# A two-layer cross-attention and FFN kernel: two engines' work in another order in each attention slot, and another opening

## The chip, the cores and the metric

The kernel runs on one NeuronCore of a Trainium2 chip, in one launch. The metric is the device time of that launch in microseconds (us). The engines are PE (TensorE, the matrix engine), DVE (VectorE), ACT (ScalarE), POOL (GpSimd) and SP (SyncE, which here only issues DMA transfers). Each runs its own list of instructions in program order, and they meet at semaphores: an instruction adds to a counter when it is done, and a `wait_ge` holds an engine's list until a counter has a value. TensorE's clock has two levels, 1.2 and 2.4 GHz; the profile gives the granted one as a share of the full one.

## The reference

Eight batches of 256 tokens with 128 features go through two layers. Every sublayer reads the layer norm of the residual x and is added to x.

```python
x = x + L0_xattn(_layernorm(x), ctx_1024, ctx_1024, ...)   # 16 heads of 8 features, 256 x 256 scores per head
x = x + L0_ffn(_layernorm(x), ...)                         # 8 experts, top 1 by a softmax gate: silu(x W1 + b1) W2 + b2
x = x + L1_xattn(_layernorm(x), ctx_1024, ctx_1024, ...)   # 16 heads, no biases, position bias slope * distance, mask
x = x + L1_ffn(_layernorm(x), ...)                         # square(relu(x W_fc.T)) W_proj.T, then 5 spiking steps
```

One attention, cut down:

```python
wq, wk, wv = (q @ Wq.T + bq), (k @ Wk.T + bk), (v @ Wv.T + bv)      # split into 16 heads of 8
probs = softmax(einsum('bthd,bshd->bhts', wq, wk) / sqrt(8))
out = einsum('bhts,bshd->bthd', probs, wv).reshape(b, t, d) @ Wo.T + bo
```

## The kernel before

The order in time is: loads and an opening, the attention of layer 0, the gate and the sorting of tokens by expert, the experts, the attention of layer 1, the second FFN. The two attentions are one piece of code (`attention_on_tensor`, `attention_on_scalar`, `attention_on_vector`, `attention_on_gpsimd`, `attention_on_sync`), built with `ly["bias"]` true for layer 0 and `ly["position"]` true for layer 1.

**Slots.** An attention is a software pipeline written out by hand. `slots_loop` calls `slot_fn` for the slots s = -3 to 8. In slot s, batch b = s is `cur` (its second score pass, the exponentials and the products with the values), batch s + 1 is `nxt` (its first score pass and the maxima over keys), the projections of batch s + 2 are made (`new`), and the output of batch s - 1 is finished (`old`). Nothing but this hand-written order, on each engine, and the semaphores set who goes first. `new` ends with slot 5, `nxt` with slot 6.

**A slot on PE.** `pair(0)` to `pair(7)` are the score products of two heads each, of `nxt` (line 292, into S1) and of `cur` (line 301, into S2). Between them stand: `m_turn` (line 352, turns the row maxima `mparts` so that they can be written as rows of the query tile), `pv` (line 343, probabilities times values, four groups per batch; group 3 of a batch falls into the next slot), the turn of the outputs `Osb` (line 382), the turn of the normed x (line 406), the query product (415), the key product (421), the turn of the normalised output `attn` (426), the output projection (434) and the value product (445). Small results share two PSUM banks, M[0] and M[1], which is why many of them wait for the copy of the one before.

**A slot on ACT.** `exp(0)` to `exp(7)` (line 508) read S2. Between them ACT copies small results out of PSUM: `m_copy` (516), `o_copy` (495), `xnT` (532), `qf` and `q_hi` (538, 543: the queries in float32 and their float16 high part), `kf` and `k_hi` (479, 484, in `keys_on_scalar`), `aT` (558) and the values `Vt` (568).

**DVE and POOL.** DVE makes the 16 maxima of `nxt` (line 651, two per `r(i)`), turns them into `mparts` in layer 0 (`shift`, line 659), normalises outputs (`o_norm`), adds the projected output to X (740), and makes the sums of the layer norm. POOL takes the norm's root (627), applies the norm (620), makes the low parts `q_lo` and `k_lo` (805, 763), and in layer 0 adds the output bias to X (815). In layer 1 POOL makes `mparts` from the maxima in five steps (`parts`, 775 to 783), and in slots 0 to 3 `mix_on_gpsimd` (1330, 1333) adds the experts' result for batch s + 4 to X, as the last thing of the slot.

**Opening.** SP loads the context, the key weights, the first two batches of X in one transfer, the query weights, then the other six batches and two more weights; ACT loads `qkb` (biases), `eye`, `rows` and `ob`. Six of these count into `loaded`. PE and DVE wait for all six. DVE clears tiles first, then scales the biases and makes the norm's sums; POOL clears `pos_parts` (needed in slot 4), applies the norm of the first batches and makes `q_lo` of batch 0. The first score products need the whole query tile of batch 0, whose low part is the last to arrive.

Of the kernel before, what the change touches and what calls it, by code (L numbers as in the profile page):

```python
# [33 lines left out]
P = 128  # L34
# [71 lines left out]
def build(nc, t, out):  # L106

    with ExitStack() as ctx:
# [75 lines left out]
        loaded, loaded_x, loaded_late, pos_stored = sem("loaded"), sem("loaded_x"), sem("loaded_late"), sem("pos_stored")  # L184
        inited, zeroed = sem("inited"), sem("zeroed")
        N_LOADS, N_LOADS_X, N_LATE = 6, 4, 22
        N_PARTS_MADE = 8
        INIT_KEYS, INIT_TILES, INIT_SECOND, N_INIT = 14, 17, 22, 25
# [95 lines left out]

        def attention_on_tensor(pe, ly, masked, ffn=None):
# [50 lines left out]
            def pv(b, par, g):  # L336
# [19 lines left out]
            def slot_fn(b, par, s):  # L356
# [51 lines left out]
                if ly["bias"]:  # L408
                    outputs_turn()
# [7 lines left out]
                pair(3)  # L417
                if new and not keys_ahead(ly, s):
# [73 lines left out]
        def attention_on_scalar(act, ly, ffn=None):  # L492
# [5 lines left out]
            def slot_fn(b, par, s):  # L498
# [20 lines left out]
                if cur and ly["bias"]:  # L519
                    m_copy(b, 1)  # L520
# [4 lines left out]
                if cur and ly["position"]:  # L525
                    m_copy(b, 1)
# [1095 lines left out]
```

## Time and profile before

| | |
|---|---|
| median of three runs | 433.56 us (433.47 to 438.4) |
| the profiled execution | 437.06 us |
| its span in the trace | 434.8 us |
| mean granted clock of TensorE | 0.872 |
| PE busy | 338.6 us (78%) |
| DVE busy | 297.0 us (68%) |
| ACT busy | 253.3 us (58%) |
| POOL busy | 152.4 us (35%) |

The span starts with the first instruction and ends with the last. Busy times include overlap with other engines, so no share by itself says what ends a stage. Per stage, read as "what did the engine that is waited for wait for", the chain of waits and the idle time before each instruction tell more.

### The profile page before, as it was taken

The numbers are of one execution on the slowest core, as the hardware profiler recorded it, in microseconds if no ns is written. First come the engines' busy times: TensorE is split into PE (matmuls) and PEld (weight loads), VectorE is DVE, ScalarE is ACT, GpSimd is POOL, SyncE is SP. The second block draws the span as 40 slices with busy tenths as digits, with TensorE's granted clock in tenths as the row PEclk, the third lists the DMA queues.
The fourth block names the chain that finished last, engine by engine and source line by source line (L and its number), as shares of the span: only waits on it lengthen the run. The fifth ranks groups of instructions, "written<-read, shape, count | busy, mean of one in ns | idle before, by whom it ended". The sixth has DMA issues, their size and how long they took to land.

```text
span 434.8 us, 9212 instructions
## 1 busy us (share of the span) xinstructions
PE 338.6 (78%) x3164; PEld 195.4 (45%) x3164; DVE 297.0 (68%) x762; ACT 253.3 (58%) x436; POOL 152.4 (35%) x255
## 2 busy tenths in 40 slices
PE   1499998879988934999941759889789888968882
PEld 0133344434443522998940213434434443457771
DVE  5677888888774666466614766878787873238885
ACT  2128878877668310665521137768777867457772
POOL 3431333245200205654027364445354210444500
PEclk9999999999888765899985555998998978789997
DMA  4214432333111041354212122112111100000001
GB/s 145 60 55 136 139 85 90 98 84 80 59 54 55 11 149 34 112 158 123 45 51 66 51 64 68 29 51 60 49 32 58 56 5 6 2 2 0 24 26 48
DMA packets 36062, 27.37 MB, mean 63 GB/s; under 512 B 6080, under 2 KB 32064, under 8 KB 36016
## 3 DMA queue, kind: packets, MB, share of 16 engines
q1 hardware_dynamic: 33040, 23.55, 18.7%
q0 software_dynamic: 1248, 2.56, 2.8%
q10 hardware_dynamic: 1728, 0.66, 0.6%
q8 instruction: 28, 0.46, 0.4%
q14 instruction: 18, 0.15, 0.1%
HBM read 14.22 MB, written 4.13 MB: 42 GB/s over the span
## 4 chain that ended last, share of the span: by engine, by line
PE 48%; DVE 20%; POOL 10%; issue 10%; ACT 6%; DMA 4%; SPq 1%; POOLq 0%; ACTq 0%; DVEq 0%
PE M L343 11%; DVE nm L651 9%; PE S L292 9%; PE S L1232 5%; PE S L1251 5%; PE M L434 3%; PE M L445 2%; DVE tmp L1364 2%; PE M L415 2%; POOL xn L620 2%; PE M L352 2%; DVE Pt L1367 2%; POOL w_ff L1148 2%; PE M L1420 1%; DMA wq<-in_wq 1%
## 5 line engine op out<-in xcount | busy, mean ns | idle before, releaser
L651 DVE TENSOR_REDUCE nm<-S 128x2 f32<-128x512 f32 x256 | 164.6, 688 | 44.4 <-PE S L292 37.9
L508 ACT ACTIVATE Pt<-S 128x1024 f32<-128x1024 f32 x128 | 130.2, 1019 | 43.0 <-PE S L301 40.5
L292 PE MATMUL S<-Kt,Qt 32*128 32x256 f16 x512 | 84.8, 309 | 17.2 <-DVE nm L651 6.2
L301 PE MATMUL S<-Qt,Kt 32*128 32x256 f16 x512 | 77.5, 299 | 0.7 <-ACT Pt L508 0.7
L343 PE MATMUL M<-Pt,Vt 128*32 128x256 f32 x1024 | 76.4, 421 | 0.1
L292 PEld LDWEIGHTS S<-Kt,Qt 32*128 32x128 f16 x512 | 23.1, 95 | 79.3 <-DVE nm L651 53.9
L627 POOL TENSOR_TENSOR rstd<-ve,mhalf 128x2 f32<-128x2 f32 x24 | 17.5, 728 | 67.9 <-DVE ve L605 67.7
L343 PEld LDWEIGHTS M<-Pt,Vt 128*32 128x32 f32 x1024 | 28.7, 117 | 27.6 <-issue 13.6
L1279 ACT ACTIVATE hf<-S,b1c 128x128 f32<-128x128 f32 x92 | 26.3, 368 | 18.3 <-PE S L1232 17.0
L805 POOL TENSOR_TENSOR q_lo<-qf,q_hi 128x256 f16<-128x256 f32 x15 | 10.2, 678 | 67.5 <-ACT q_hi L543 49.5
L1141 POOL DMA_INDIRECT xt<-normed_x,source x23 | 22.2, 967 | 20.1 <-PE M L1242 13.5
L1232 PE MATMUL S<-x_t,w_t 128*128 128x128 f32 x184 | 27.0, 293 | 0.7 <-DVE x_t L1302 0.5
L1251 PE MATMUL S<-w_ff,hf 128*128 x184 | 24.3, 276 | 0.9 <-issue 0.9
L301 PEld LDWEIGHTS S<-Qt,Kt 32*128 32x128 f16 x512 | 21.7, 95 | 6.3 <-ACT Pt L508 3.8
L1232 PEld LDWEIGHTS S<-x_t,w_t 128*128 128x128 f32 x184 | 23.8, 202 | 1.7 <-issue 1.4
L532 ACT ACTIVATE xnT<-M 128x256 f32<-128x256 f32 x16 | 6.1, 382 | 28.8 <-PE M L406 28.8
L1251 PEld LDWEIGHTS S<-w_ff,hf 128*128 128x128 f32 x184 | 22.4, 192 | 1.2 <-issue 1.2
L1148 POOL DMA_INDIRECT w_ff<-sorted_y,slot x16 | 15.6, 974 | 20.5 <-DMA sorted_y<-ysb 16.2
L620 POOL TENSOR_SCALAR xn<-X,mv,rstd 128x128 f32<-128x128 f32 x28 | 22.2, 798 | 1.4
L434 PE MATMUL M<-wo,aT 128*128 128x128 f32 x64 | 13.8, 348 | 8.7 <-ACT aT L558 8.7
L516 ACT ACTIVATE mT<-M 64x256 f16<-64x256 f16 x32 | 11.9, 373 | 14.1 <-PE M L352 14.1
L352 PE MATMUL M<-eye,mparts 128*64 128x128 f16 x64 | 10.4, 251 | 12.2 <-POOL mparts L783 8.9
(174 smaller groups left out, 542.6 us busy)
## 6 DMA issues: line engine op xcount, KB each, us to landing
w_ff<-in_w SPq DMA_DIRECT2D x8, 512.0 KB, 4.0
ctxT<-in_ctxT SPq DMA_DIRECT2D x16, 128.0 KB, 2.6
Pt<-in_mask SPq DMA_DIRECT2D x8, 256.0 KB
Qt<-q_hi SPq DMA_DIRECT2D x28, 64.0 KB, 1.9
Kt<-k_hi SPq DMA_DIRECT2D x28, 64.0 KB, 1.9
sorted_y<-ysb SPq DMA_DIRECT2D x23, 64.0 KB
Kt<-k_lo SPq DMA_DIRECT2D x16, 64.0 KB, 1.9
Qt<-q_const SPq DMA_DIRECT2D x16, 64.0 KB, 3.5
```

The lines of the kernel that those rows point to most:

```text
L292: mm = pe.matmul(S1[h % 2][:, q, :], Qt[b % NBUF][rows_of(h), h // HG, q * P:(q + 1) * P], Kt[b % NBUF][rows_of(h), h // HG, :], start=Tru ...
L301: mm = pe.matmul(S2[pair % 2][:, hh, k, :], Kt[b % NBUF][rows_of(h), h // HG, k * P:(k + 1) * P], Qt[b % NBUF][rows_of(h), h // HG, :], st ...
L343: mm = pe.matmul(M[1][KB * i:KB * i + KB, tile * S:(tile + 1) * S], Vflat[par][:, at:at + KB], Pt[g][:, i, k * S:(k + 1) * S], start=(sub ...
L434: mm = pe.matmul(M[1][:, q * D:(q + 1) * D], aT[:, q * P:(q + 1) * P], W["o", ly["index"]][:, :], start=True, stop=True)
L508: act.activation(Pt[i // 2][:, 2 * j:2 * j + 2, :].rearrange("p a n -> p (a n)"), S2[i % 2][:, :, :, :].rearrange("p a k n -> p (a k n)"), ...
L620: i = pool.tensor_scalar(xn[par][:, q, :], X[:, b * QT + q, :], mv[:, q, 0:1], rstd[:, q:q + 1], ALU.subtract, ALU.mult)
L651: v.tensor_reduce(nm[par][:, h // 8, :, h % HG, h // HG % 2], S1[h % 2][:, :, :], AX.X, ALU.max, negate=True)\
L1141: pool.indirect_dma_start(xt[j % XT_BUFS][:, :], None, xn_dram, bass.IndirectOffsetOnAxis(ap=source[:, j:j + 1].bitcast(U32), axis=0)) \
L1148: pool.indirect_dma_start(yg[:, i, :], None, ys_dram, bass.IndirectOffsetOnAxis(ap=slot[:, i:i + 1].bitcast(U32), axis=0)) \
L1232: mm = pe.matmul(S2[j % H_BUFS // 2][:, j % 2, c // 2, (c % 2) * P:(c % 2 + 1) * P], w1_t[j % X_BUFS][:, c, :], x_t[j % X_BUFS][:, :], sta ...
L1251: pe.matmul(o, hf[j % HF_BUFS][:, c * P:(c + 1) * P], second_weights(e, c), start=(c == 0), stop=False)
L1279: i = act.activation(hf[j % HF_BUFS][:, c * P:(c + 1) * P], S2[j % H_BUFS // 2][:, j % 2, c // 2, (c % 2) * P:(c % 2 + 1) * P], ACT.Silu, ...
```

## The change

The table of the slots is changed in five places, the opening in four.

- PE, layer 0: `m_turn(b, 1)` goes behind `pv(b - 1, 3)`, as it stood in layer 1; ACT's `m_copy(b, 1)` goes behind `o_copy` with it. The turn of the outputs goes ahead of that of the normed x.
- PE, both layers: the turn of `attn` goes ahead of the key product. ACT, both layers: the copy `aT` goes ahead of `kf` and `k_hi`.
- The last batch's `pv` accumulates in M[0] and waits for the maxima's copy, no longer for `x_added`.
- POOL, layer 1: `mix_on_gpsimd` stands right behind `parts(b, 1)` at the start of the slot instead of at its end.
- Opening: X of batch 0 is SP's first transfer, X of batch 1 another; the key weights and `rows` come first on ACT's queue, `qkb` fourth; `loaded` counts five transfers. DVE makes the norm's sums of batch 0 before it waits for `loaded`, applies the norm of batches 0 and 1 and makes `q_lo` of batch 0. POOL clears the value tiles `Vt` (`clear_values`) instead of DVE, and clears `pos_parts` behind slot 0 of layer 0 (`clear_positions`).

The core of the diff:

```diff
-        INIT_KEYS, INIT_TILES, INIT_SECOND, N_INIT = 14, 17, 22, 25
+        INIT_KEYS, INIT_TILES, INIT_SECOND, N_INIT = 12, 15, 19, 21
...
+        def o_bank(b):
+            return M[0] if b == B - 1 else M[1]
...
                 if cur:
-                    if old:
+                    if s == B - 1:
+                        pe.wait_ge(ly["mT_copied"], 2 * B)
+                    elif old:
                         pe.wait_ge(ly["x_added"], b)
...
         def first_tiles_on_vector(v):
+            v.wait_ge(loaded, 16 * N_LOADS)
+            v.tensor_scalar(qkbs[:, 0:1], qkb[:, 0:1], QK / float(np.sqrt(DH)), None, ALU.mult).then_inc(inited, 1)
+            v.tensor_scalar(qkbs[:, 1:2], qkb[:, 1:2], QK, None, ALU.mult).then_inc(inited, 1)
             v.tensor_scalar(Kt[0][:, :, :], Kt[0][:, :, :], rows[:, 0:1], None, ALU.add).then_inc(inited, 1)
+            v.tensor_scalar(vb[:, :], ones32[:, :], qkb[:, 2:3], None, ALU.mult).then_inc(inited, 1)
...
+                    if s == -3 and ly["bias"]:
+                        first_tiles_on_vector(v)
                     if s < -1:
                         norm_apply(v, b + 3, xn[1 - par], ly["xrstd"], ly["xn_ready"])
+                    if s == -3 and ly["bias"]:
+                        v.wait_ge(loaded_x1, 16)
+                        norm_sums(v, 1, ly["norm_own"])
...
+        def clear_values(pool, i):
+            pool.memset(Vt[i][:, :, :, :], 0.0).then_inc(cleared, 1)
+            pool.wait_ge(cleared, 2 * i + 1)
+            pool.memset(Vheads[i][:, :, :, DH], 1.0).then_inc(cleared, 1)
+
+        def clear_positions(pool):
+            pool.memset(pos_parts[:, :, :], 0.0).then_inc(zeroed, 1)
+            pool.wait_ge(zeroed, 1)
+            pool.memset(pos_parts[:, 0:PARTS, :], MROW).then_inc(zeroed, 1)
...
                 if cur and ly["position"]:
                     parts(b, par, 1)
+                    if s < B - MIX:
+                        mix_on_gpsimd(pool, b + MIX)
...
             first = QT * 2
+            sp.dma_start(X[:, 0:QT, :], t["x"][:, 0:QT, :]).then_inc(loaded_x0, 16)
             context_on_sync(sp, ly[0], -2, 0)
-            for dst, src in [(W["k", 0][:, :], t["wk0"]), (X[:, 0:first, :], t["x"][:, 0:first, :]), (W["q", 0][:, :], t["wq0"])]:
-                sp.dma_start(dst, src).then_inc(loaded, 16)
+            sp.dma_start(W["q", 0][:, :], t["wq0"]).then_inc(loaded, 16)
+            sp.dma_start(X[:, QT:first, :], t["x"][:, QT:first, :]).then_inc(loaded_x1, 16)
...
-            for dst, src in [(qkb[:, :], t["qkb"]), (eye[:, :], t["c_eye"]), (rows[:, :], t["c_rows"])]:
+            for dst, src in [(rows[:, :], t["c_rows"]), (W["k", 0][:, :], t["wk0"]), (eye[:, :], t["c_eye"]), (qkb[:, :], t["qkb"])]:
                 act.dma_start(dst, src).then_inc(loaded, 16)
```

ACT's list in slot 1 of layer 0, from the copy of the queries to that of the values, before:

```order
L538 ACTIVATE qf<-M,qkbs 128x256 [waits L0_q_lo,L0_q_done]
L543 ACTIVATE q_hi<-qf 128x256 [waits L0_q_tile,L0_q_copied]
L508 ACTIVATE Pt<-S_1 128x1024 [waits L0_p2_done]
L479 ACTIVATE kf<-M,qkbs 128x256 [waits L0_k_lo,L0_k_done]
L484 ACTIVATE k_hi<-kf 128x256 [waits L0_k_rep,L0_k_copied]
L558 ACTIVATE aT<-M 128x256 [waits L0_aT_done]
L508 ACTIVATE Pt<-S_0 128x1024 [waits L0_p2_done,L0_pv_done]
L568 ACTIVATE Vt<-M 128x8x4x8 [waits L0_pv_done,L0_v_done]
```

And after the change:

```order
L533 ACTIVATE qf<-M,qkbs 128x256 [waits L0_q_lo,L0_q_done]
L538 ACTIVATE q_hi<-qf 128x256 [waits L0_q_tile,L0_q_copied]
L505 ACTIVATE Pt<-S_1 128x1024 [waits L0_p2_done]
L551 ACTIVATE aT<-M 128x256 [waits L0_aT_done]
L476 ACTIVATE kf<-M,qkbs 128x256 [waits L0_k_lo,L0_k_done]
L481 ACTIVATE k_hi<-kf 128x256 [waits L0_k_rep,L0_k_copied]
L505 ACTIVATE Pt<-S_0 128x1024 [waits L0_p2_done,L0_pv_done]
L563 ACTIVATE Vt<-M 128x8x4x8 [waits L0_pv_done,L0_v_done]
```

`aT`, which PE's output projection waits for, has moved ahead of two copies; the exponential behind them has the same three copies ahead of it.

POOL's list in layer 1 from the norm of one slot to the next slot's `q_lo`, before (rows 1330 and 1333 are the mix, 775 to 783 the parts of the next slot):

```order
L620 TENSOR_SCALAR xn<-X,mv,rstd 128x128 [waits L1_xnT_done,L1_xrstd]
L620 TENSOR_SCALAR xn<-X,mv,rstd 128x128
L1330 TENSOR_TENSOR w_ff<-w_ff,gate 128x256
L1333 TENSOR_TENSOR X<-X,w_ff 128x256 [waits moe_scaled]
L775 TENSOR_SCALAR mr<-nm 128x16 [waits L1_mT_done,L1_max_done]
L777 CAST mparts<-mr 128x8x2 [waits L1_own]
L779 TENSOR_TENSOR mr<-mr,mparts 128x16 [waits L1_own]
L781 CAST mparts<-mr 128x8x2 [waits L1_own]
L783 TENSOR_TENSOR mparts<-mr,mparts 128x8x2 [waits L1_own]
L805 TENSOR_TENSOR q_lo<-qf,q_hi 128x256 [waits L1_q_hi,L1_q_tile]
```

And after:

```order
L615 TENSOR_SCALAR xn<-X,mv,rstd 128x128 [waits L1_xnT_done,L1_xrstd]
L615 TENSOR_SCALAR xn<-X,mv,rstd 128x128
L783 TENSOR_SCALAR mr<-nm 128x16 [waits L1_mT_done,L1_max_done]
L785 CAST mparts<-mr 128x8x2 [waits L1_own]
L787 TENSOR_TENSOR mr<-mr,mparts 128x16 [waits L1_own]
L789 CAST mparts<-mr 128x8x2 [waits L1_own]
L791 TENSOR_TENSOR mparts<-mr,mparts 128x8x2 [waits L1_own]
L1343 TENSOR_TENSOR w_ff<-w_ff,gate 128x256
L1346 TENSOR_TENSOR X<-X,w_ff 128x256 [waits moe_scaled]
L818 TENSOR_TENSOR q_lo<-qf,q_hi 128x256 [waits L1_q_hi,L1_q_tile]
```

The five steps now stand ahead of the mix.

DVE's list in the opening of layer 0, from the norm of batch 0 to the tiles of the other buffers, after the change (before, `xn` and `q_lo` are not on DVE, and the wait for `loaded` stands ahead of the norm's sums):

```order
L597 BN_AGGR mv<-st 128x2 x2
L600 TENSOR_SCALAR ve<-mv 128x2 [waits L0_norm_own]
L627 TENSOR_SCALAR qkbs<-qkb 128x1 [waits loaded]
L628 TENSOR_SCALAR qkbs<-qkb 128x1
L629 TENSOR_SCALAR Kt<-Kt,rows 128x1024
L630 TENSOR_SCALAR vb<-ones,qkb 128x128
L631 TENSOR_SCALAR q_const<-q_const,rows 32x1024
L605 TENSOR_SCALAR xn<-X,mv,rstd 128x128 [waits L0_xrstd]
L605 TENSOR_SCALAR xn<-X,mv,rstd 128x128
L588 BN_STATS st<-X 128x6 [waits loaded_x1]
```

`xn` of batch 0 is made on DVE behind five instructions that wait for the loads.

## Rows read from the trace of the kernel before

**Rows 1.** The page, part 1: engine, busy us (share of the span), instructions.

```profile
PE 338.6 (78%) x3164; PEld 195.4 (45%) x3164; DVE 297.0 (68%) x762; ACT 253.3 (58%) x436; POOL 152.4 (35%) x255
```

**Rows 2.** The chain that ended last, both openings: start us, us, what.

```profile
2.11 5.62 DMA wq<-in_wq
...
10.17 1.59 POOL xn L620 x2
15.23 0.80 POOL q_lo L805
16.05 1.93 DMA Qt<-q_lo
...
236.19 0.43 DVE q_lo L708
```

**Rows 3.** The DMA view, 0 to 20 us: issues, sizes, us to landing.

```profile
ob<-in_ob ACTq DMA_DIRECT2D x1, 64.0 KB, 5.5
...
rows<-in_c_rows ACTq DMA_DIRECT2D x1, 1.5 KB, 3.4
```

**Rows 4.** The timeline of the opening: start us, us, engine, line, operation.

```profile
0.72 1.80 POOL L1506 MEMSET pos_parts<- 128x2048 f16 x1 [0.29 <-POOLq L1615]
...
10.04 1.28 ACTq L490 DMA_DIRECT2D Kt<-k_hi  x2
...
12.54 0.38 ACT L532 ACTIVATE xnT<-M 128x256 f32<-128x256 f32 x1 [2.52 <-PE M L406]
...
14.73 0.42 ACT L543 ACTIVATE q_hi<-qf 128x256 f16<-128x256 f32 x1
...
18.02 0.61 PE L292 MATMUL S<-Kt,Qt 32*128 32x256 f16 x4 [3.41 <-DMA Qt<-q_lo]
```

**Rows 5.** The timeline of ACT, layer 0, slots 1 and 2.

```profile
55.67 0.38 ACT L568 ACTIVATE Vt<-M 128x256 f32<-128x256 f32 x1 [0.33 <-PE M L445]
...
68.04 0.37 ACT L558 ACTIVATE aT<-M 128x256 f32<-128x256 f32 x1
```

**Rows 6.** The timeline of PE, layer 0, slot 2.

```profile
61.07 0.27 PE L352 MATMUL M<-eye,mparts 128*64 128x128 f16 x2 [0.23 <-DVE mparts L659]
...
68.45 0.71 PE L434 MATMUL M<-wo,aT 128*128 128x128 f32 x4 [0.72 <-ACT aT L558]
```

**Rows 7.** Who waited for whom, PE, 46 to 146 us: us in total, times, longest.

```profile
PE M L434 <- ACT aT L558: 4.3, 6, 0.7
PE M L352 <- DVE mparts L659: 1.8, 4, 1.1
```

**Rows 8.** The timeline of DVE and POOL around the ends of slots 0 and 3 of layer 0.

```profile
46.71 0.18 DVE L659 TENSOR_SCALAR mparts<-nm 128x16 f16<-128x16 f32 x1
...
88.38 1.38 DVE L659 TENSOR_SCALAR mparts<-nm 128x16 f16<-128x16 f32 x1
...
88.78 0.96 POOL L1074 MEMSET b2rows<- 128x1024 f16 x1
```

**Rows 9.** The timeline of layer 1 around the start of slot 4.

```profile
315.10 2.63 DVE L651 TENSOR_REDUCE nm<-S 128x2 f32<-128x512 f32 x4
...
318.20 0.74 POOL L1333 TENSOR_TENSOR X<-X,w_ff 128x256 f32<-128x256 f32 x1
319.03 0.20 POOL L775 TENSOR_SCALAR mr<-nm 128x16 f32<-128x16 f32 x1
...
320.53 0.27 PE L352 MATMUL M<-eye,mparts 128*64 128x128 f16 x2 [1.35 <-POOL mparts L783]
...
321.15 2.49 DVE L651 TENSOR_REDUCE nm<-S 128x2 f32<-128x512 f32 x4 [1.27 <-PE S L292]
```

**Rows 10.** The timeline of PE: one group of `pv` at either clock.

```profile
142.26 1.94 PE L343 MATMUL M<-Pt,Vt 128*32 128x256 f32 x16
...
315.01 1.07 PE L343 MATMUL M<-Pt,Vt 128*32 128x256 f32 x16
```

**Rows 11.** One stretch: window, length, busy us of PE, PEld, DVE, ACT, POOL; clock; DMA.

```profile
267.00:270.00 3.00, 3.00 (x31) 1.06 (x34) 1.69 (x7) 1.72 (x4) 0.88 (x2) 0.50 0.33 96
```

More of the change, by code:

```diff
@@ L391, in slot_fn @@
                     ffn_start(ffn, -2)
-                if ly["position"]:
-                    maxima_turn()
+                if cur:
+                    pe.wait_ge(ly["v_copied"], b + 1)
+                    m_turn(b, par, 1)
                 pair(1)
-                if ly["position"]:
-                    outputs_turn()
+                if old:
+                    pe.wait_ge(ly["o_copied"], b)
+                    if s == B:
+                        pe.wait_ge(ly["x_added"], B - 1)
+                    for n in range(QT * NPK):
+                        q, tile = n // NPK, n % NPK
+                        mm = pe.transpose(M[1][:, n * P:(n + 1) * P], Osb[par1][:, tile, q * P:(q + 1) * P], eye[:, :])
+                    mm.then_inc(ly["ot_done"], 1)
                 if new:
@@ L417, in slot_fn @@
                 pair(3)
+                if old:
+                    pe.wait_ge(ly["ot_norm"], b)
+                    for q in range(QT):
+                        mm = pe.transpose(M[1][:, q * P:(q + 1) * P], attn[:, q, :], eye[:, :])
+                    mm.then_inc(ly["aT_done"], 1)
                 if new and not keys_ahead(ly, s):
@@ L524, in slot_fn @@
                     ffn_start(ffn, -2)
-                if cur and ly["position"]:
+                if cur:
                     m_copy(b, 1)
@@ L548, in slot_fn @@
                 exp(3)
-                if new and not keys_ahead(ly, s):
-                    keys_on_scalar(act, ly, b, nxt)
                 gate = s == B and ly["bias"]
@@ L560, in slot_fn @@
                     gate_copies(act, 2, GATE_AHEAD)
+                if new and not keys_ahead(ly, s):
+                    keys_on_scalar(act, ly, b, nxt)
                 exp(4)
@@ L563, in slot_fn @@
                     act.wait_ge(ly["v_done"], b + 2)
-                    if b == -1:
-                        act.wait_ge(inited, N_INIT)
+                    if b <= 0 and ly["bias"]:
+                        act.wait_ge(cleared, 2 * (b + 2))
                     if old:
@@ L694, in slot_fn @@
                     v.wait_ge(loaded_x, 16 * N_LOADS_X)
-                if ly["position"] and s < 0:
-                    if s == -1:
+                if s < 0:
+                    if s == -1 and ly["position"]:
                         add_experts(v, 2)
@@ L712, in slot_fn @@
                     norm_sums(v, b + 3, ly["norm_own"])
-                elif ahead:
-                    norm_stats(v, b + 3, ly["norm_own"], ly["xvar"], applied(b + 3))
-                if s == -3 and ly["bias"]:
-                    first_tiles_on_vector(v)
                 if s == -1 and ly["bias"]:
@@ L821, in slot_fn @@
                     gather(pool, 2 * QT + 8, NT)
-                if ly["position"] and 0 <= s < B - MIX:
-                    mix_on_gpsimd(pool, b + MIX)
             def slot_and_small_parts(b, par, s):
                 slot_fn(b, par, s)
+                if s == 0 and ly["bias"]:
+                    clear_positions(pool)
                 if s == 3 and ly["bias"]:
@@ L1505, in _ @@
         def _(pool):
-            pool.memset(pos_parts[:, :, :], 0.0).then_inc(zeroed, 1)
-            pool.wait_ge(zeroed, 1)
-            pool.memset(pos_parts[:, 0:PARTS, :], MROW).then_inc(zeroed, 1)
+            clear_values(pool, 0)
             attention_on_gpsimd(pool, ly[0])
```

49 lines of the change are left out of this document (12 added, 37 removed).

## The prediction

> **What bounds the kernel now.** I read the page's busy shares first [rows 1]. No engine is full: PE 78% of the span, DVE 68%. So an idle gap that sits on the path is worth its length, and busy work taken off an engine is worth nothing by itself. Then I read the chain of waits, which names what ended last, stage by stage, and then the timeline around each instruction that moves. Three places matter.
>
> In the opening the chain is one serial string: the loads until 7.73 (2.11 + 5.62), the norm and its application on POOL (1.59), the low part of the queries on POOL (0.80) and its transfer (1.93) [rows 2], and the first score products start at 18.02 [rows 4].
>
> In a slot of layer 0 PE stands still twice: 0.23 before the turn of the maxima and 0.72 before the output projection [rows 6]. Over the layer the first makes 1.8 us in 4 waits, one of them 1.1, the second 4.3 us in 6 [rows 7].
>
> In layer 1 the turn of the maxima waits 1.35 for POOL, and DVE then waits 1.27 for PE [rows 9].
>
> **The opening.** Call T the moment when `loaded` is complete, 7.7 before. Behind T ACT's list decides, and both ends of each step are in rows 4. ACT issues two transfers from 10.04 for 1.28 (to 11.32), and only then copies `xnT`; before, that copy starts at 12.54, since POOL's `xn` ends at 11.76 (10.17 + 1.59) [rows 2]. After, DVE makes `xn`. In front of it stand five instructions behind `loaded`, for which I take about 1.2 us (an estimate from their sizes: two of them are passes over float16 tiles like the ones cleared here), and the two halves take about 0.5, so `xn` is there at T + 1.7, the turn on PE at T + 2.5, and ACT is free at T + 3.6. The copy starts there instead of at T + 4.8: a gain of 1.2. The second step is `q_lo`. It ran from 15.23 to 16.03 on POOL, behind a `q_hi` that ended at 15.15. DVE does the same subtraction in layer 1's opening in 0.43 [rows 2] instead of 0.80, a gain of 0.3, of which the other two transfers, which ACT issues, leave all but a little: second issue plus 1.9 us lands within 0.1 of it. Sum 1.5.
>
> T itself: the query weights move one place forward, but `qkb` becomes ACT's fourth transfer, in the place of `ob`, which took 5.5 us from an issue at 2.14 and so landed at 7.6; the third, `rows`, took 3.4 [rows 3]. So T lies between some 5.5 (as quick as `rows`) and 7.7 (as `ob`). The transfer of 768 KB that slowed `ob` keeps its place, so I take the late end, 7.4: a gain of 0.3, with 2.2 as the other end. DMA: Bandwidth & Descriptors of the Trainium skill (Queues, rings and completion order) says that a semaphore's increment lands only after every earlier write of that DMA engine, on all its queues. By that, a 1.5 KB transfer issued here lands no sooner than a 64 KB one; `ob`'s row agrees, and the gain would be 0.
>
> What moved to POOL in the opening is hidden: its memset of 2048 columns took 1.80 and started at 0.72 [rows 4]; the one of 1152 columns of float32 costs between 1.0 (by columns) and 2.0 (by bytes), and POOL has nothing to do before the root at T or so. If the second clearing is late, the value copy of slot -1, ten microseconds later, covers it. DVE's tiles for the other buffers now stand behind `q_lo`; they take some 2.7 us, and end just as the first maxima become possible. Opening: **-1.8**.
>
> **Layer 0.** First, `aT`. ACT makes `kf` and `k_hi` first and starts `aT` at 68.04 [rows 5]; PE waits until 68.45 for it [rows 6]. With `aT` first PE's 0.72 goes. What is late next is the exponential behind it: it has the same three copies ahead of it and so starts at the same time, and the value copy `Vt` comes after it. That copy had waited 0.33 for PE [rows 5]. So only 0.33 of the 0.72 reaches the end of the slot. This holds in slots 1 to 5, where key products exist; slot 7 has only the wait, which stays. 5 x 0.33 = 1.65. `k_hi` comes 0.37 later, and SP waits for it; but SP is issuing the query's transfers until then, and its own keys are wanted over 4 us later, so I take 0.
>
> Second, the turn of the maxima behind `pv`. The 0.23 waits and the slack of the exponential give 0.15 in each of the other slots, some 6 x 0.15 = 0.9. The long one is of another kind: `mparts`, a DVE instruction of 0.18, took 1.38 in slot 4 and ended at 89.76, as POOL's memset did (88.78 + 0.96) [rows 8]. With a `pv` of 1.07 [rows 10] ahead of it, PE's 1.1 us are hidden: 0.9.
>
> Third, a cost. `clear_positions` now puts 1.80 + 0.74 us of memset on POOL right where slot 1 begins, and `mparts` of slot 1 at 46.71 [rows 8] falls into it. By the row of slot 4 it ends when the memset does. The turn waits 0.4 beyond `pv` if only for the first memset, 1.2 if for both; I take 0.7, and between 0 and 1.2 for the range. SBUF — State Buffer of the Trainium skill (Who interferes with whom) says the same: GpSimd and a VectorE instruction that needs the shared port pair exclude each other for a whole instruction. It speaks against this move. The two slot-4 rows agree.
>
> The turn of the outputs ahead of the norm's gives DVE its input 0.4 earlier, but now waits for `o_copied` some 0.2: 0. Layer 0: -1.65 - 0.9 - 0.9 + 0.7 = **-2.75**.
>
> **Layer 1.** The maxima of slot 4 are complete at 317.73 (315.10 + 2.63), but POOL is in the mix until 318.94 and starts `parts` at 319.03; PE turns at 320.53 [rows 9]. With `parts` first it starts at about 317.8, 1.2 earlier. PE's `pv` ends at 319.2, so the turn comes right behind it. DVE's 1.27 of idle time [rows 9] lets it follow, and ACT was idle too, so the 1.2 survives to the second exponential. The mix falls at the ends of slots 0 to 3; slot 1's `parts` were late by DVE and not by the mix, so three slots gain: 3 x 1.2 = 3.6. The mix itself (1.4 us) now lies in POOL's idle 4.5 us before `q_lo`, and DVE's sums need the mix of the slot before. In slot 0 it waits for the gathered rows, beside nothing. `aT` as in layer 0: 5 x 0.33 = 1.65. The last batch's bank removes a wait that was nearly over: 0. Layer 1: **-5.25**.
>
> Sum: -1.8 - 2.75 - 5.25 = **-9.8 us**. Made against the profiled execution, 437.06 (span 434.8) to 427.3. That execution was 3.5 above the median, by TensorE's clock, I take it, and the saving does not depend on that: 433.56 - 9.8 = **423.8**. About 2% (8.7 us) is what a measurement of this kernel can tell from no change.
>
> **Rivals.**
>
> *Half of it is given back (428.5).* PE and DVE hand the two S1 banks to and fro, and DVE has only about 1 us free in a slot of 14. If the small gains of 0.15 and 0.33 are lost there (all of 2.55 in layer 0 and 1.65 in layer 1) and the stall of slot 1 takes 1.2, then 9.8 - 4.2 - 0.5 = 5.1 is left: 428.5. For it: DVE's gaps are short. Against it: two of them, in front of the sum and of the next maxima, are just those that `aT` ends. Chance 0.22.
>
> *The clock falls less often, or T comes early (419.5).* TensorE's granted clock falls to half several times in both attentions, after slots in which PE had idle time, and `pv` then takes 1.94 instead of 1.07 [rows 10]. A slot has four of them. If one slot in each layer keeps its clock, some 2 us each; with T at 5.5, 2.2: 423.8 - 4.3 = 419.5. TensorE: Matmul & The Clock Gate of the Trainium skill (Part 1) says that activity releases the clock; the gaps removed here would help. Chance 0.16.
>
> *The clock stays at half for longer (over 433.6: slower).* Layer 1 starts at half clock, with PE busy in 3.00 of 3.00 us at 267 to 270 and the clock at 0.50 of the full one [rows 11]. If the new phase of the work moves that release by slots, each slot costs at least 4 x 0.87 for `pv` [rows 10] and some 2 for projections, 5.5 us less 1 of slack, 4.5. From 9.8 / 4.5 = 2.2 slots on, the gain is gone; three slots give 437, and 442.3, a loss of 2%, needs four. For it: that stretch is 48 us long already. Against it: PE gets busier, not idler. Chance 0.04.
>
> *The change doesn't do what it says.* The opening could be tied to another load and the mix to its gathers, so that only the `aT` terms are left, -3.3: 430. Chance 0.05.
>
> **How the numbers follow.** The forecast has 0.53, with its own range of 421.5 to 426.5 from the bounds of T (-1.9, +0.3), of the memset (-0.7, +0.5) and of the slots. The range of all reaches to both neighbours: 418.5 to 430; above and below lie the slower case and the tails. Faster by over 2% means under 424.9: most of the forecast (0.38) and the clock case (0.16), 0.54. Slower by over 2%: half of the slow case, 0.02. Within: 0.44.
>
> **What the profile after would show.** First score products at about 16.2, with `xnT` behind ACT's two transfers; `loaded` ended by a transfer on ACT's queue; the output projection without its wait for `aT` in slots 1 to 5, and `Vt` without its wait for PE; no wait of 1.1 for `mparts` in slot 4, but one in slot 1 beside the memset; in layer 1 `parts` right behind the maxima and slots 2 to 4 shorter by 1.5. Wrong would be: slots of unchanged length with the waits elsewhere (DVE for S1, ACT for `o_copied`), or a longer stretch at half clock.

## The result and the profile after

The changed kernel takes 420.64 us (median of four runs, 419.66 to 423.13) against 435.7 for the kernel before in the same comparison: a ratio of 0.966, 95% interval 0.9575 to 0.9746, so 11 to 18.5 us faster. Measured again beside three other kernels it took 421.16, ratio 0.968 (0.963 to 0.974). The ratios leave out two single runs that lie over 1.5% above the fastest of their kernel: 432.35 of `p_keys` and 441.24 of the kernel before. The profiled execution took 419.95 (span 417.8, mean granted clock 0.887), that of before 437.06.

The page, part 1, of the changed kernel, answers to [rows 1]: PE and DVE have nearly the same work (4.1 and 2.4 us less busy time) in a span that is 17 us shorter.

```profile
PE 334.5 (80%) x3164; PEld 193.5 (46%) x3164; DVE 294.6 (71%) x763; ACT 250.2 (60%) x436; POOL 151.0 (36%) x254
```

**The opening** [rows 2 to 4]. The chain of the changed kernel (start, length, what), and then its timeline:

```profile
2.14 3.81 DMA qkb<-in_qkb
...
12.81 2.06 DMA Qt<-q_hi
```

```profile
7.08 0.59 DVE L605 TENSOR_SCALAR xn<-X,mv,rstd 128x128 f32<-128x128 f32 x2
...
8.27 1.28 ACTq L487 DMA_DIRECT2D Kt<-k_hi  x2
...
9.59 0.38 ACT L527 ACTIVATE xnT<-M 128x256 f32<-128x256 f32 x1 [1.36 <-PE M L403]
...
12.24 0.42 DVE L710 TENSOR_TENSOR q_lo<-qf,q_hi 128x256 f16<-128x256 f32 x1 [1.31 <-ACT q_hi L538]
...
14.91 0.61 PE L297 MATMUL S<-Kt,Qt 32*128 32x256 f16 x4 [3.24 <-DMA Qt<-q_hi]
```

`loaded` is complete at 5.95 (2.14 + 3.81), not at 7.73. Behind it `xnT` starts 3.64 later, behind ACT's two transfers, and the first scores 8.96 later, where before it was 10.29. So of the 3.11 gained, 1.8 are T and 1.3 what follows it.

**A slot of layer 0** [rows 5, 6]: ACT, DVE and PE in slot 2.

```profile
64.68 0.38 ACT L551 ACTIVATE aT<-M 128x256 f32<-128x256 f32 x1
...
65.11 0.71 PE L429 MATMUL M<-wo,aT 128*128 128x128 f32 x4
...
66.05 0.41 DVE L738 TENSOR_TENSOR X<-M,X 128x256 f32<-128x256 f32 x1
66.63 1.29 DVE L648 TENSOR_REDUCE nm<-S 128x2 f32<-128x512 f32 x2 [0.17 <-PE S L297]
66.67 0.38 ACT L563 ACTIVATE Vt<-M 128x256 f32<-128x256 f32 x1
67.11 0.30 PE L357 MATMUL M<-eye,mparts 128*64 128x128 f16 x2 [0.50 <-ACT Vt L563]
```

PE's output projection and ACT's `Vt` have no brackets now: nobody waits there. PE has a new wait, 0.50 for `Vt` in front of the turn of the first half of the next batch's maxima. (The other turn has none in slots 1 and 2, at 59.49 and 72.77. It waits for `v_copied` where it waited for `mT_copied`, an edit that the list of the change doesn't name.) Over the layer (PE's waits from 40 to 142: total, times, longest; compare [rows 7]):

```profile
PE M L357 <- ACT Vt L563: 2.5, 5, 0.5
PE M L416 <- DVE attn L668: 2.1, 7, 0.3
...
PE M L429 <- ACT aT L551: 0.7, 1, 0.7
```

**The start of slot 1**, where POOL's memset now lies beside `mparts` [rows 8]:

```profile
43.35 1.81 POOL L763 MEMSET pos_parts<- 128x2048 f16 x1
...
44.89 0.30 DVE L656 TENSOR_SCALAR mparts<-nm 128x16 f16<-128x16 f32 x1
```

`mparts` ends at 45.19, as the memset does (45.16), but PE is in `pv` until 46.3 and waits for nothing.

**Layer 1**, the starts of slot 4 and of slot 5 [rows 9]:

```profile
304.49 0.20 POOL L783 TENSOR_SCALAR mr<-nm 128x16 f32<-128x16 f32 x1 [0.53 <-DVE nm L648]
...
305.99 0.27 PE L357 MATMUL M<-eye,mparts 128*64 128x128 f16 x2
...
319.04 0.26 PE L297 MATMUL S<-Kt,Qt 32*128 32x256 f16 x1 [1.27 <-DMA Qt<-mT]
```

POOL now waits 0.53 for DVE's maxima, where before it was still in the mix when they were complete, and PE's turn has no wait. But slot 5 begins with a wait that before had none: 1.27 for the transfer of the maxima's row, which the chain has with 4.02 us.

**Where the time went.** The start of the output projection marks each slot. The table has, for the two profiled executions, the lead of the changed kernel there, and the length of the slots (a star marks one that holds more than 1 us at half of TensorE's full clock).

| | lead, us | slots before | slots after |
|---|---|---|---|
| first scores | 3.11 | | |
| layer 0, slot 1 | 2.64 | | |
| slots 1 to 5 | 6.34 | 13.97, 13.99, 14.86, 13.98 | 13.27, 13.28, 13.28, 13.27 |
| slots 5 to 8 | 8.40 | 14.46\*, 12.74\*, 12.80\* | 13.07, 12.72\*, 12.15\* |
| layer 1, slot 1 | 9.95 | | |
| slots 1 to 5 | 15.58 | 15.24\*, 14.90, 14.92, 14.93\* | 13.26, 13.25, 13.26, 14.59 |
| slots 5 to 8 | 17.20 | 13.12, 13.81\*, 13.59\* | 13.20\*, 13.19\*, 12.51\* |

Laid out in order of time, the lead of the two profiled executions grows by 3.1 in the opening, shrinks by 0.5 until slot 1, grows by 5.8 from slot 1 to 8 of layer 0, by 1.6 until slot 1 of layer 1, and by 7.25 from there to slot 8. The opening and the slots that hold no such stretch in either kernel (1 to 5 of layer 0, 2 to 4 of layer 1) make 3.1 + 3.7 + 3.3 = 10.1 us; in the rest the clock may have a part. The forecast had nothing for the 1.6 between slot 8 of layer 0 and slot 1 of layer 1.

### The profile page after: what moved, and what is told of

Its sections match the earlier page's. It is cut to its first block, busy times and chain, and to the rows that moved or that the text cites. A ratio compares the mean times of both kernels' runs of the same rounds, so it can differ in the third digit from the quotient of the medians.

```text
span 417.8 us, 9215 instructions
## 1 busy us (share of the span) xinstructions
PE 334.5 (80%) x3164; PEld 193.5 (46%) x3164; DVE 294.6 (71%) x763; ACT 250.2 (60%) x436; POOL 151.0 (36%) x254
## 3 DMA queue, kind: packets, MB, share of 16 engines
HBM read 14.22 MB, written 4.13 MB: 44 GB/s over the span
## 4 chain that ended last, share of the span: by engine, by line
PE 45%; DVE 16%; ACT 12%; issue 10%; DMA 7%; POOL 5%; SPq 2%; ACTq 1%; POOLq 0%; DVEq 0%
PE M L348 13%; PE S L297 10%; ACT Pt L505 5%; PE S L1245 4%; PE S L1264 4%; DVE nm L648 3%; DVE tmp L1377 3%; DVE Pt L1380 2%; DMA Qt<-q_const 2%; DMA sorted_y<-ysb 2%; PE M L410 2%; POOL w_ff L1161 2%; PE M L1433 2%; PE M L357 1%; PE M L440 1%
## 5 line engine op out<-in xcount | busy, mean ns | idle before, releaser
L297 PE MATMUL S<-Kt,Qt 32*128 32x256 f16 x512 | 86.0, 305 | 16.2 <-DMA Qt<-q_hi 7.1
L348 PE MATMUL M<-Pt,Vt 128*32 128x256 f32 x1024 | 74.9, 414 | 0.2
L615 POOL TENSOR_SCALAR xn<-X,mv,rstd 128x128 f32<-128x128 f32 x24 | 19.0, 798 | 1.2
L1377 DVE SCALAR_TENSOR_TENSOR tmp<-Pt 128x256 f32<-128x256 f32 x32 | 13.7, 428 | 7.1 <-ACT Pt L1477 6.3
L1321 DVE COPY ysb<-S 128x128 f32<-128x128 f32 x23 | 6.6, 288 | 16.6 <-PE S L1265 8.3
```

The source lines that it names most:

```text
L297: mm = pe.matmul(S1[h % 2][:, q, :], Qt[b % NBUF][rows_of(h), h // HG, q * P:(q + 1) * P], Kt[b % NBUF][rows_of(h), h // HG, :], start=Tru ...
L348: mm = pe.matmul(o_bank(b)[KB * i:KB * i + KB, tile * S:(tile + 1) * S], Vflat[par][:, at:at + KB], Pt[g][:, i, k * S:(k + 1) * S], start= ...
L615: i = pool.tensor_scalar(xn[par][:, q, :], X[:, b * QT + q, :], mv[:, q, 0:1], rstd[:, q:q + 1], ALU.subtract, ALU.mult)
L1377: v.scalar_tensor_tensor(tmp[:, :], mem[par][:, k - 1, :], BETA, mem[par][:, 0, :], ALU.mult, ALU.add) \
```

## The experiments

**One part at a time.** Four kernels start from the one before.

`p_keys` moves these lines of PE ahead of the key product, and `keys_on_scalar` on ACT behind `aT`:

```diff
+                if old:
+                    pe.wait_ge(ly["ot_norm"], b)
+                    for q in range(QT):
+                        mm = pe.transpose(M[1][:, q * P:(q + 1) * P], attn[:, q, :], eye[:, :])
+                    mm.then_inc(ly["aT_done"], 1)
                 if new and not keys_ahead(ly, s):
                     pe.wait_ge(ly["q_copied"], b + 3)
```

> The kernel before with one part of the change: the turn of attn ahead of the key product on PE, aT ahead of kf and k_hi on ACT, in both layers. Theory A (the prediction's term): 0.33 of the 0.72 survives in each of 10 slots, -3.3 us, slots of layer 0 shorter by 0.33. Theory B (the whole wait survives, because the value copy's place in the queue was never the next limit): 0.7 in each of 10 slots, -7 us, slots of layer 0 of 13.3 instead of 13.98. If the slots stay at 13.98, both fall.

Measured: 426.8 (425.89 to 432.35) against 435.6, ratio 0.979 (0.973 to 0.985), a gain of 6 to 12. Ordinary slots of layer 0 take 13.27 and 13.28 instead of 13.98; in layer 1 14.15 and 14.26 instead of 14.90. Theory B: all of the wait survives. Why, is to be seen in slot 2. The timeline of ACT and DVE there, before:

```profile
66.31 1.01 ACT L508 ACTIVATE Pt<-S 128x1024 f32<-128x1024 f32 x1
...
68.30 1.02 ACT L508 ACTIVATE Pt<-S 128x1024 f32<-128x1024 f32 x1
...
69.20 0.42 DVE L740 TENSOR_TENSOR X<-M,X 128x256 f32<-128x256 f32 x1 [0.52 <-PE M L434]
...
69.97 1.29 DVE L651 TENSOR_REDUCE nm<-S 128x2 f32<-128x512 f32 x2 [0.34 <-PE S L292]
```

And in `p_keys`:

```profile
65.45 1.01 ACT L508 ACTIVATE Pt<-S 128x1024 f32<-128x1024 f32 x1
...
66.83 0.71 PE L434 MATMUL M<-wo,aT 128*128 128x128 f32 x4
...
67.44 1.00 ACT L508 ACTIVATE Pt<-S 128x1024 f32<-128x1024 f32 x1
67.77 0.41 DVE L740 TENSOR_TENSOR X<-M,X 128x256 f32<-128x256 f32 x1
68.35 1.29 DVE L651 TENSOR_REDUCE nm<-S 128x2 f32<-128x512 f32 x2 [0.17 <-PE S L292]
```

From one exponential to the next it is 1.99 in both: on ACT nothing is gained there, as I had said. But DVE's sum, which before waited 0.52 for the projection, and the maxima behind it come 0.76 earlier behind the same exponential (2.90 instead of 3.66). So the 0.71 follows DVE's string. In front of the turn of the maxima `p_keys` has PE's wait for `Vt` already (0.45 at 55.51).

`p_turns`, layer 0 alone:

```diff
                 pair(0)
-                if ly["bias"]:
-                    maxima_turn()
                 if old:
                     pv(b - 1, par1, 3)
...
-                if ly["position"]:
-                    maxima_turn()
+                maxima_turn()
                 pair(1)
-                if ly["position"]:
-                    outputs_turn()
+                outputs_turn()
...
-                if ly["bias"]:
-                    outputs_turn()
```

> The kernel before with one part: in layer 0 the turn of the maxima behind pv (m_copy behind o_copy) and the turn of the outputs ahead of that of the normed x. Theory A (the prediction's terms): 0.15 in each of 6 slots and 0.9 in slot 4, -1.8 us. Theory B (only the stall of slot 4 counts, ordinary slots end with the wait for aT as before): -0.9 us, ordinary slots of layer 0 unchanged at 13.98 and slot 4 at 13.98 instead of 14.86.

Measured: 432.19 (430.65 to 436.02), ratio 0.993 (0.986 to 1.000). Ordinary slots take 13.70 and 13.72, 0.27 less, slot 4 takes 13.85, 1.0 less: theory A, a little larger. PE's wait for `aT` stayed what it was in these slots, 0.73 where it was 0.72, and was 0.86 in one: alone, the turn gains in front of that wait and doesn't need the other part. From slot 1 to 2 it takes 15.01: from 55 to 59 TensorE was granted 0.57, and that stretch cost 1.3.

`p_mix`:

```diff
                     parts(b, par, 1)
+                    if s < B - MIX:
+                        mix_on_gpsimd(pool, b + MIX)
...
-                if ly["position"] and 0 <= s < B - MIX:
-                    mix_on_gpsimd(pool, b + MIX)
```

> The kernel before with one part: POOL's mix behind parts in layer 1. Theory A (the prediction's term): three slots shorter by 1.2, -3.6 us. Theory B (the trace after: four slots of layer 1 shorter by 1.65 to 1.98, of which aT has 0.33 to 0.7): four slots by 1.3, -5.2 us. Rival C: without aT's part the slot ends late anyway, under -2 us.

Measured: 430.56 (427.99 to 432.52), ratio 0.988 (0.982 to 0.994), a gain of 2.5 to 8. From slot 2 to 3 and from 3 to 4 it takes 13.70 where 14.90 was: 1.2 each, as said. From 1 to 2 it takes 14.99, with a stretch at half clock in it (281 to 285). From 4 to 5, where no mix stood in the way, it takes 13.70 in `p_turns` and `p_open` too. Theory A.

`p_open` has the whole opening of the change and the slots of before (its last slot keeps one wait of the change, for `x_added`).

> The kernel before with the whole opening of the change (order of the loads, DVE's norm and low part, POOL's clearings, so the memsets of pos_parts at the start of slot 1) and nothing else. The turn of the maxima of slot 1 stands ahead of pv here, with nothing to hide a stall. Theory A (the prediction: mparts ends with the memset beside it): opening -1.8 or, with the T of the trace after, -3.1, and slot 1 longer by 0.7 plus the 1.07 of pv, 1.4 to 1.8: -0.1 to -1.7 us in all. Theory B (the memset costs the maxima nothing): slot 1 unchanged, -3.1 us, first scores at 14.9.

Measured: 434.49 (431.31 to 437.26), ratio 0.997 (0.990 to 1.005). The first scores come at 14.85, 3.2 earlier, but at slot 1's output projection only 1.79 is left. Its start of slot 1:

```profile
43.33 1.81 POOL L775 MEMSET pos_parts<- 128x2048 f16 x1
```

```profile
43.90 1.27 DVE L668 TENSOR_SCALAR mparts<-nm 128x16 f16<-128x16 f32 x1
...
45.31 0.27 PE L357 MATMUL M<-eye,mparts 128*64 128x128 f16 x2 [0.99 <-DVE mparts L668]
```

`mparts`, otherwise 0.18, ends at 45.17, the memset at 45.14. Theory A: the stall is there, 0.99 on PE and 1.4 at the projection. The time alone could not have told it from theory B, with an interval from 4.5 us faster to 2 slower.

**What ends `loaded`.** `t_qkb5` issues `ob` fourth and `qkb` fifth:

```diff
-            for dst, src in [(rows[:, :], t["c_rows"]), (W["k", 0][:, :], t["wk0"]), (eye[:, :], t["c_eye"]), (qkb[:, :], t["qkb"])]:
+            for dst, src in [(rows[:, :], t["c_rows"]), (W["k", 0][:, :], t["wk0"]), (eye[:, :], t["c_eye"])]:
...
             for dst, src in [(ob[:, :], t["ob"].partition_broadcast(P))]:
                 act.dma_start(dst, src).then_inc(loaded_x, 16)
+            act.dma_start(qkb[:, :], t["qkb"]).then_inc(loaded, 16)
```

> The changed kernel with one edit: ACT issues ob fourth and qkb fifth. Asks what ends loaded (5.94 in the changed kernel, by qkb, 3.81 us after its issue). Theory A (place: what is issued fifth, at about 2.6, lands as ob did, 6.1 later): loaded ends at 8.7, first scores at 17.7. Theory B (a transfer of 1.5 KB is quick wherever it stands, 3.8 after its issue): loaded at 6.4, first scores at 15.4.

`t_biglate` issues the 768 KB of X behind `wv` and `wo`:

```diff
-            for dst, src in [(X[:, first:NT, :], t["x"][:, first:NT, :]), (W["v", 0][:, :], t["wv0"]),
-                             (W["o", 0][:, :], t["wo0"])]:
+            for dst, src in [(W["v", 0][:, :], t["wv0"]), (W["o", 0][:, :], t["wo0"]),
+                             (X[:, first:NT, :], t["x"][:, first:NT, :])]:
```

> The changed kernel with one edit: SP issues the 768 KB of X behind wv and wo, at about 3.5 instead of 2.6. Theory A (that transfer slows those issued just before it): qkb lands 0.5 to 1 earlier, loaded at about 5.2, first scores at about 14.2. Theory B (qkb's 3.81 are its own queue's, rows, wk and eye ahead of it): loaded stays at 5.9, first scores at 14.9.

The chains of the two, one after the other, and then from the DMA view `ob` in `t_qkb5`, fourth with the same transfers ahead of it as `qkb` in the changed kernel, and in `t_biglate`, fifth:

```profile
2.62 6.52 DMA qkb<-in_qkb
```

```profile
2.14 3.25 DMA qkb<-in_qkb
```

```profile
ob<-in_ob ACTq DMA_DIRECT2D x1, 64.0 KB, 4.7
```

```profile
ob<-in_ob ACTq DMA_DIRECT2D x1, 64.0 KB, 3.4
```

`qkb` is 1.5 KB in both. Fifth, 0.48 later in its issue, it lands 3.2 later, at 9.14, and the first scores start at 18.12, as late as before the change (426.02 us in one run). With the large transfer later it lands at 5.39, first scores at 14.43 (421.3 in one run). Theory A twice. With the changed kernel's order it landed at 5.81 to 6.44 in six executions, with the large transfer later at 5.20 to 5.39 in three (`v1` and `v2` have it too). `ob` shows the same: 64 KB took 4.7 in fourth place, 6.1 in fifth in the changed kernel, and 3.4 in fifth with the large transfer later. So the place, and above all whether the 768 KB are issued ahead of it or behind, is worth more than the size: between 1.5 and 64 KB in the fourth place lie 0.4 to 1.0.

**What the memsets cost in the whole change.** `u_clear` puts them back at the start of POOL's list:

```diff
             clear_values(pool, 0)
+            clear_positions(pool)
             attention_on_gpsimd(pool, ly[0])
...
-                if s == 0 and ly["bias"]:
-                    clear_positions(pool)
```

> The changed kernel with one edit: the memsets of pos_parts back at the start of POOL's list, behind the first clearing of Vt. Theory A (the prediction's term: they cost slot 1 of layer 0 something between 0.4 and 1.2): slot 1 shorter by 0.7. Theory B (mparts ends with the first memset, but pv hides it): mparts takes 0.18 instead of 0.30 and slot 1 is unchanged within 0.1; the opening is unchanged too, since DVE and POOL have nothing to do until loaded.

Measured: 418.29 in one run. The turn of slot 1 starts 1.00 behind the start of its `pv`, at 46.39, as in the changed kernel (46.23 behind 45.23), and slots 1 to 8 have the lengths of the table within 0.15. So the cost was 0 in the changed kernel. But in `t_biglate`, whose first two `pv` in slot 0 took 1.07, it appeared:

```profile
44.86 0.27 PE L357 MATMUL M<-eye,mparts 128*64 128x128 f16 x2 [0.97 <-DVE mparts L656]
```

`b_turn`, further down, has it too, 0.98, with no `pv` of slot 0 over 1.07, and `u_bank` 0.35 with one of 1.69. In the changed kernel the first two took 1.94:

```profile
38.85 1.94 PE L348 MATMUL M<-Pt,Vt 128*32 128x256 f32 x16
41.27 1.94 PE L348 MATMUL M<-Pt,Vt 128*32 128x256 f32 x16
43.48 1.07 PE L348 MATMUL M<-Pt,Vt 128*32 128x256 f32 x16
```

TensorE comes to its full level somewhere in slot 0. The level is read off the `pv` here, 1.94 or 1.07 as in [rows 10], for the profile's clock column has 1.00 for all of the first 110 us. It comes during or after the second `pv` in the changed kernel, in `u_clear` and in `t_qkb5`, before the first in `t_biglate` and `b_turn`. If it comes late, the maxima of slot 1 are late as well: in the changed kernel DVE starts `mparts` 1.54 behind POOL's memset, in `t_biglate` 0.41 ahead of it. One delay covers the other.

**What holds a slot at 13.26**, the same in both layers. `b_turn`:

```diff
-                if nxt:
-                    m_turn(b + 1, par1, 0)
                 if cur:
                     pv(b, par, 0)
+                if nxt:
+                    m_turn(b + 1, par1, 0)
...
+                exp(5)
+                if nxt:
                     m_copy(b + 1, 0)
-                exp(5)
```

> The changed kernel with one edit: the turn of the maxima's first half stands behind pv group 0 on PE, and its copy behind exp(5) on ACT. It asks what holds the slots of both layers at 13.26. Theory A (PE's wait of 0.5 for the value copy): slots shorter by 0.3 to 0.5, some 5 us in all against the changed kernel. Theory B (the loop between PE and DVE over S1, or the rows of the maxima, which now land 1.4 later): slots unchanged, or in layer 1 longer by up to 1, with PE waiting for the transfer of mT at each slot's start.

Measured: 419.74 (418.14 to 422.34), ratio 0.963 (0.956 to 0.971): not told apart from the change. Two slots of layer 0 take 12.89, so the wait for `Vt` was worth 0.38 there, but the two between them take 13.78 and 13.45. PE's waits, layer 0 and then layer 1:

```profile
PE S L297 <- DMA Qt<-mT: 1.6, 2, 1.0
```

```profile
PE S L297 <- DMA Qt<-mT: 3.4, 4, 1.2
```

Both theories hold, one against the other: the row of the maxima is issued later, and what was gained is waited for.

**Versions that might beat both.** Beside them the changed kernel once more:

> The changed kernel unchanged, to have it beside the next three on the same chip: 420.6 within 1.5 us. It also tests whether two things of its trace are of the kernel or of one execution. The long start of slot 5 in layer 1 (a period of 14.59 instead of 13.26, for the transfer of mT): theory A (a property of the order) expects it again, theory B (chance) a period of 13.26. TensorE's release in slot 0 of layer 0 at 43.4: if it comes ahead of the first pv (38.9), the turn of slot 1 waits some 1.0 for mparts and slot 1 still starts 0.9 earlier.

Measured: 421.16 (419.66 to 422.81). Slot 5 of layer 1 began late again, 14.22; `u_bank` has 14.48 there, `t_biglate` 14.31, `u_clear` 14.08, `t_qkb5` 13.26 with a wait of 0.5 elsewhere. It belongs to the order, though its size varies. TensorE's level rose late in slot 0 again (`pv` of 1.94 at 39.41 and 1.77 at 41.82, 1.07 from 43.86), and slot 1 had no wait for `mparts`.

`v1` has the edits of `t_biglate` and `u_clear` and two more:

```diff
                     act.activation(xnT[:, :], M[0][:, 0:S], ACT.Copy).then_inc(ly["xnT_copied"], 1)
+                    if s == -2 and ly["bias"]:
+                        act.wait_ge(inited, INIT_TILES)
+                        first_keys_out(act, ly)
...
             sp.dma_start(tile[1:P:4, :, :], k_lo[:, :]).then_inc(ly["k_rep"], 16)
+            between()
             if ly["position"]:
...
-                        keys_on_sync(sp, ly, b, nxt)
-                if nxt:
+                        keys_on_sync(sp, ly, b, nxt, (lambda: rows_of_maximum(b + 1, 0)) if nxt else (lambda: None))
+                if nxt and (not new or keys_ahead(ly, s)):
                     rows_of_maximum(b + 1, 0)
```

`first_keys_out` issues the two transfers of `k_hi`, which stood ahead of `xnT`; `between` issues the row of `mT`, which stood behind that of the positions.

> The changed kernel with four edits: the 768 KB of X behind wv and wo; the memsets of pos_parts at the start of POOL's list; ACT issues the two transfers of the first k_hi behind the copy xnT instead of ahead of it; SP issues the row of mT ahead of that of the positions. Theory A (the terms as measured: 0.5 for the first, 0 to 1.0 for the second, by when TensorE's clock is released in slot 0, 1.0 for the third, 0.7 of the 1.3 in slot 5 of layer 1 for the fourth): first scores at 13.4 to 13.9, total 2 to 3.5 us below the changed kernel, 417 to 418.5. Rival B (the opening's gain is lost while the clock is at half in slot 0, released at the same 43.4): under 1 us.

Measured: 420.01 (416.77 to 421.75), ratio 0.9645 (0.960 to 0.969). The first scores come at 13.28, 1.6 to 2.1 earlier than in the two executions of the change, and the lead of 2.5 at slot 1 lasts until slot 5. Then it goes: from slot 6 to 7 and 7 to 8 it takes 13.56 and 13.38 instead of 12.72 and 12.15, with TensorE at half from 115 to 122 (in the changed kernel from 118.6 to 121.7) and again from 138 on, where the changed kernel, at half from 132 to 136, kept its full clock until 145. Windows (length, busy us of PE, PEld, DVE, ACT, POOL, granted clock, DMA) of `v1` and of the changed kernel, first around 117 and then around 140:

```profile
117.00:118.00 1.00, 1.00 (x12) 0.68 (x11) 0.42 (x1) 0.13 (x1) 0.00 (x0) 0.50 0.00 0
```

```profile
117.00:118.00 1.00, 0.70 (x8) 0.23 (x8) 0.96 (x4) 0.53 (x2) 0.00 (x0) 1.00 0.32 127
```

```profile
138.00:146.00 8.00, 7.82 (x38) 7.44 (x39) 5.11 (x21) 2.69 (x7) 0.55 (x1) 0.53 0.37 112
```

```profile
136.00:145.00 9.00, 7.83 (x75) 5.42 (x74) 5.16 (x22) 4.20 (x9) 2.61 (x1) 1.00 0.14 45
```

Slot 5 of layer 1 takes 13.27: the earlier issue of `mT`'s row removed that wait. The total is 1.2 below the change, within the scatter. The total fits the rival, with another place: in its one trace the opening's lead is gone in the last slots of layer 0, not in slot 0, and these are the slots with more time at half clock.

`v2` is `v1` with the edit of `b_turn`.

> The same four edits, and the turn of the maxima's first half behind pv group 0, its copy behind exp(5). Theory A (the turn's place gives 0.38 in each slot whose mT lands in time; with mT ahead of the positions it does): 2 to 4 us below v1. Theory B (mT is issued over a microsecond later and now the row of the positions waits for it as well): PE waits at the starts of slots, same as v1 or up to 3 us slower.

Measured: 419.91 (417.63 to 421.38), ratio 0.963 (0.959 to 0.967). Theory B: PE waits 2.4 us in two slots of layer 1 for the row of the positions, which now stands behind `mT`'s, and 1.5 in one of layer 0 for `mT`'s own. No version beats the change by what the runs can tell.

`u_bank` has the last batch's `pv` in M[1] again, behind `x_added`:

```diff
-            return M[0] if b == B - 1 else M[1]
+            return M[1]
```

> The changed kernel with one edit: the last batch's pv back in M[1], waiting for x_added. Theory A (the prediction's term): 0, the period from slot 7 to 8 unchanged within 0.15. Theory B (the trace after: that period fell from 12.80 to 12.15 in layer 0 and from 13.59 to 12.51 in layer 1, while p_keys without the bank has 12.92 and 13.63): 0.6 in each layer comes back.

Measured: 419.77 in one run; from slot 7 to 8 it takes 12.16 in layer 0 and 12.71 in layer 1, against 12.15 and 12.51. Theory A, with 0.2 in layer 1 that one run can't place.

## Why the prediction was right, and where its sizes were off

Forecast 423.8, measured 420.64: right in sign and within the whole range of 418.5 to 430, but below the forecast's own one (421.5 to 426.5), nearer to the clock rival's 419.5. The gain was 9.8 by the forecast, 15.1 by the medians of the comparison and 17.1 by the two profiled executions. By these, layer 0 gave 5.3 and not 2.75 from the first scores on, and layer 1 7.25 and not 5.25. Most of the mechanisms appeared where I had put them; the size of T and of `aT` was off, and the memsets' cost did not appear.

*The opening, -1.8: measured -3.1.* "The second step" and the copy behind ACT's two transfers were right: `xnT` at T + 3.64 (said 3.6), 1.3 gained behind T (said 1.5). The term T was mis-sized: 1.8 and not 0.3. I took `ob`'s 5.5 us as the price of the fourth place, but the lists ahead of that place had changed too: in `t_qkb5` the same `ob` takes 4.7 there. What ended `loaded` before was `wq`, fourth on SP's queue with 5.62 [rows 2], and it is third now and no longer the last. The 768 KB that I blamed for `ob` are worth 0.6 to `qkb` (3.81 against 3.25 in `t_biglate`). The order of landings agrees with what I had cited from the Trainium skill, DMA: Bandwidth & Descriptors (Queues, rings and completion order): in `t_qkb5` the 1.5 KB land at 9.14, behind the 768 KB issued 0.04 ahead of them, at 8.3. My reading of it, a gain of 0, did not follow, since it says nothing of how long the earlier writes take. Why they took less is open, and no run splits the 256 KB of X alone or moves `wk` alone. In the middle of the loads the DMA engines' busy share (the last but one number) was lower before than after:

```profile
5.00:6.00 1.00, 0.00 (x0) 0.00 (x0) 0.00 (x0) 0.00 (x0) 0.00 (x0) 1.00 0.37 98
```

```profile
5.00:6.00 1.00, 0.01 (x1) 0.01 (x1) 0.03 (x1) 0.00 (x0) 0.07 (x1) 1.00 0.68 175
```

*Layer 0, `aT`: 0.33 in a slot, measured 0.71.* The step that failed is "What is late next is the exponential behind it": true on ACT, but it asked one engine. PE and DVE hand S1 to and fro, and behind the same exponential DVE's sum and maxima came 0.76 earlier. *The turn behind `pv`*: 0.15 was 0.27 alone, and nothing beside the `aT` edit: slots take 13.27 with both (the changed kernel) and with `aT` alone (`p_keys`). So these two parts don't add. (The totals alone couldn't show it: by the medians the four parts gained 8.8, 3.4, 5.1 and 1.1, 18.4 in sum, and together 15, but each of these is uncertain by some 3 us.) *Slot 4*: 14.06 in `p_keys`, 13.28 in the change, so 0.8 for the turn there, where I said 0.9.

*The memsets, +0.7: measured 0, and 0.35 to 0.98 where the clock was early.* The mechanism was as told: in `p_open`, `t_biglate`, `b_turn` and `u_bank` DVE's `mparts` ends within 0.03 us of the memset. SBUF — State Buffer of the Trainium skill (Who interferes with whom) has such an exclusion too, and these rows agree. What I had not asked was when the maxima of slot 1 would be ready.

*Layer 1*: the mix 1.2 a slot, measured 1.2 alone. With `aT` 1.65 a slot, where I said 1.5: the sum of two measured parts would be 1.9. Not foreseen was the late row of `mT`, which cost 1.3 once. Before, 3.76 us lay between its issue and the start of slot 5 (330.15 to 333.91); after, a slot leaves 2.92 (301.52 to 304.44 at slot 4, without a wait), and at slot 5 the transfer took 4.02. So the shorter slots took 0.8 of its slack; why this one takes longer than the one before it is open. The bank: 0, as said.

*The clock*, a rival that I gave 0.16, may have its part in the total. (Its 4.3 us were also not the sum of the terms named, 2 x 2 and 1.9 more from T, 5.9.) Layer 1 came to the full level at 261.6 and not at 272, 10.4 earlier where the lead was 8.2 (its first scores at 231.63 and 239.86), and between 275 and 400 the time at half clock adds up to 24 us before and 14 after. In the scatter of the kernel before, over 25 of its runs, time and mean granted clock go together (correlation -0.87; 432.45 us at 0.888, 441.24 at 0.869), which doesn't say which of the two leads. How much of the 15 us is due to the clock, the runs don't separate. As an estimate, the stretch of 3.4 us at half in `p_turns` cost 1.3; at that price the 10 us fewer between 275 and 400 would be worth up to 4.

## What to carry to other kernels

When a wait goes, follow every engine that meets behind it, not only the one that was late: here nothing was gained between two of ACT's exponentials, and the slot still got shorter by the whole wait, through DVE. Time each part of a change alone as well as all together: parts that shorten the same loop share one floor, here 13.27 until `b_turn` moved the wait for `Vt`. And at each removal ask which transfer is issued last and how much slack it has; here the row of `mT` became the next wait.

## What the runs showed of the hardware that was not expected

A transfer of 1.5 KB took 3.81 us from issue to landing in ACT's fourth place (`after`), and 6.52 in the fifth, behind the issue of 768 KB on the other queue (`t_qkb5`). A DVE instruction of 0.18 us took 1.27 (`p_open`) and 2.24 (`t_biglate`) beside a POOL memset of 1.8, each time ending within 0.03 of it; in `t_biglate` its record starts 0.41 ahead of the memset's and it is held all the same:

```profile
42.47 2.24 DVE L656 TENSOR_SCALAR mparts<-nm 128x16 f16<-128x16 f32 x1
...
42.88 1.80 POOL L763 MEMSET pos_parts<- 128x2048 f16 x1
```

And TensorE's rise to full level in slot 0 came behind none, one or two `pv` groups in kernels of nearly the same order. At 0.87 for each group (1.94 less 1.07), a gain in front of it can be lost in it.
